# Mask products, two normalisations and a rank rule moved between engines in a two-layer graph kernel

## What is computed

```python
# layer 0, three convolutions, per graph
h = h @ W + b
nh = h / max(norm(h), 1e-12)
ew = adj * (nh @ nh.T)
h = ew @ h                      # relu after the first two

# layer 1 starts with a sequential thinning of the adjacency, row by row
num = sum(row)
sf = (num + 1) // 2 if num > 10 else 1
rank = cumsum(row)
rm = row & (rank % sf == 0)     # only where the node is valid and num > 1
carry[n, :] &= ~rm
carry[:, n] &= ~rm
```

## Time and profile before

| | |
|---|---|
| median of three runs | 2725.25 us (2724.58 to 2729.75) |
| profiled execution, its own time | 2730.12 us |
| its span | 2728.3 us |
| granted TensorE clock, mean | 0.988 |
| busy over the span: PE | 2589.2 us (95%) |
| PE weight loads | 1639.6 us (60%) |
| DVE | 2156.8 us (79%) |
| ACT | 1301.0 us (48%) |
| POOL | 838.1 us (31%) |

### The profile page before, as it was taken

How to read it: one execution, slowest core, us unless ns; L and a number is a source line. 1 busy time by engine, 2 the same in 40 slices (tenths; PEclk the granted TensorE clock), 3 DMA queues, 4 the chain that set the end, 5 groups by cost and what they waited for, 6 DMA issues and landing times. The chain is left out here.

```text
span 2728.3 us, 38640 instructions
## 1 busy us (share of the span) xinstructions
PE 2589.2 (95%) x12390; PEld 1639.6 (60%) x12390; DVE 2156.8 (79%) x5387; ACT 1301.0 (48%) x3804; POOL 838.1 (31%) x449
## 2 busy tenths in 40 slices
PE   7999989999897998989999998999999999999898
PEld 5666656656554665656665554555555555555797
DVE  5889999989889888889989967766666635776676
ACT  3657536555553665455653411322223344444576
POOL 0000050210255003031102120866666613343663
PEclk9999999999998999999999999999999999999999
DMA  7264184363286347056327134355555519997663
GB/s 242 78 182 130 44 196 146 86 183 106 62 208 165 84 124 214 14 156 190 97 86 193 39 72 146 117 198 195 200 200 200 201 62 346 401 401 284 239 233 154
DMA packets 325876, 455.46 MB, mean 167 GB/s; under 512 B 155680, under 2 KB 218528, under 8 KB 325664
## 3 DMA queue, kind: packets, MB, share of 16 engines
q1 hardware_dynamic: 325664, 452.89, 51.9%
HBM read 352.13 MB, written 67.11 MB: 154 GB/s over the span
## 5 line engine op out<-in xcount | busy, mean ns | idle before, releaser
L730 PE MATMUL a_acc<-a_ew,a_Hr 128*128 128x512 f32 x1536 | 752.8, 602 | 0.0
L569 POOL TENSOR_TENSOR a_kp<-a_T,stage 128x512 fp8e4<-128x512 fp8e4 x216 | 275.8, 1288 | 1332.5 <-DMA stage<-a_T 747.1
L900 DVE TENSOR_TENSOR a_ew<-adj,a_cos 128x512 f32<-128x512 f32 x768 | 507.4, 680 | 60.7 <-PE a_cos L723 59.1
L721 PE MATMUL a_cos<-a_nh 128*128 128x512 f32 x768 | 418.5, 545 | 29.4 <-DVE a_ew L900 20.3
L730 PEld LDWEIGHTS a_acc<-a_ew,a_Hr 128*128 128x128 f32 x1536 | 276.7, 191 | 161.1 <-issue 113.4
L835 ACT ACTIVATE a_v<-a_D,a_wb,a_small 128x256 f16<-128x256 f32 x512 | 288.0, 634 | 104.1 <-PE a_D L763 100.6
L825 ACT ACTIVATE a_vr<-a_D,a_small 128x128 f16<-128x128 f32 x560 | 210.5, 458 | 208.1 <-DVE a_small L977 207.6
L723 PE MATMUL a_cos<-a_nh,a_nl 128*128 128x512 f32 x768 | 307.1, 400 | 0.0
L722 PE MATMUL a_cos<-a_nl,a_nh 128*128 128x512 f32 x768 | 304.8, 397 | 0.0
L1385 PE MATMUL b_acc<-adj,b_z 128*128 128x512 f32 x512 | 225.0, 592 | 0.0
L1482 PE MATMUL b_acc<-adj,b_z 128*128 128x512 f32 x512 | 222.5, 592 | 0.0
(11 more groups left out here) (269 smaller groups left out, 4344.5 us busy)
## 6 DMA issues: line engine op xcount, KB each, us to landing
adj<-in_adjT SPq DMA_DIRECT2D x108, 1024.0 KB, 12.7
adj<-in_adjT SPq DMA_DIRECT2D x128, 512.0 KB, 4.0
stage<-in_adj SPq DMA_DIRECT2D x256, 256.0 KB, 3.2
scr_keep<-a_kp SPq DMA_DIRECT2D x256, 64.0 KB, 2.0
scr_z<-b_zT SPq DMA_DIRECT2D x32, 512.0 KB, 3.9
scr_ag<-b_a SPq DMA_DIRECT2D x32, 512.0 KB, 3.2
stage<-scr_keep SPq DMA_DIRECT2D x13, 1024.0 KB, 7.9
b_kp<-scr_keep SPq DMA_DIRECT2D x12, 1024.0 KB, 8.2
```

The lines of the kernel that those rows point to most:

```text
L569: e.tensor_tensor(as_blocks(kp[c % 3][:]), row_half(slot, j, q), turned[:, :, :, :, q % 2], ALU.mult, saturate=False).then_inc(T[done], 1)
L721: e.matmul(cos[j][:], n[:, blk(k)], n[:, half(j)], start=True, stop=False)
L730: e.matmul(acc[j][:], Hr[u % 2][:, k, :], ew[idx % EW][:], start=(k == 0), stop=(k == NK - 1)).then_inc(E["agg"], 1)
L900: e.tensor_tensor(ew[idx % EW][:], adj[g % 2][:, k, half(j)], cos[j][:], ALU.mult).then_inc(E["ew"], 1)
```

## The change

Four things change, all in the first stage:

- All 256 mask products are DVE instructions; POOL has none and runs nothing in the stage. Their planned cost is 620 instead of 700 (DVE) or 1150 (POOL), their rank 3 instead of 1.
- The scaling of `hd` and of `lnb` is eight ACT instructions of 128 x 128 each with the scale (and in `lnb` the bias) as a per-partition operand, planned at 1610. DVE keeps the reciprocals and makes the bias of `lnb` with one more small instruction.
- The rule works on a quarter of the count and needs nine instructions instead of ten. The halving that one of them did is gone; `base` gets one small instruction more.
- `PACE` is 24 instead of 25, so that the dilation's blocks may start somewhat later; planned costs of `rule`, `base` and `wide` are adjusted.

```diff
-PACE = 25
+PACE = 24
...
-def masker(quad, q, j):
-    late = max(q | 1, 4 * j + 3) == NK - 1
-    return "dve" if quad > 1 and late and q % 2 else "pool"
...
-            add("dve", ("lnb", g), 2280, 1, [("act", "lna", g)] + ([("pe", "hf", 0)] if g == 1 else []))
-            add("pe", ("lnc", g), 880, 0, [("dve", "lnb", g)] + bank)
+            add("dve", ("lnb", g), 400, 1, [("act", "lna", g)])
+            add("act", ("lnb", g), 1610, 0, [("dve", "lnb", g)] + ([("pe", "hf", 0)] if g == 1 else []))
+            add("pe", ("lnc", g), 880, 0, [("act", "lnb", g)] + bank)
...
-        add("dve", ("hd", v), 1373, 1, [("act", "hc", v)])
-        add("pe", ("hf", v), 880, 0, [("dve", "hd", v)])
+        add("dve", ("hd", v), 210, 1, [("act", "hc", v)])
+        add("act", ("hd", v), 1610, 0, [("dve", "hd", v)])
+        add("pe", ("hf", v), 880, 0, [("act", "hd", v)])
...
-        add("dve", ("base", n), 190, 2, [("pe", "base", n)], None, None, "D1")
+        add("dve", ("base", n), 320, 2, [("pe", "base", n)], None, None, "D1")
...
-            add("dve", ("rule", n, r), 1290, 3, ...
+            add("dve", ("rule", n, r), 1140, 3, ...
...
-                add("act", ("wide", n, i, j), 900, 1, ...
+                add("act", ("wide", n, i, j), 960, 1, ...
...
-                        add(e, ("mask", quad, i, q, j), 1150 if e == "pool" else 700, 1, ...
+                        add("dve", ("mask", quad, i, q, j), 620, 3, ...
...
+                elif kind == "lnb":                       # ACT
+                    g, = a
+                    x = xt if g in (1, G) else tmp
+                    e.wait_ge(E["lnm"], g + 1)
+                    if g in (1, G):
+                        e.wait_ge(E["tnh"], 3 * g if g == G else 1)
+                    for k in range(NK):
+                        t = e.activation(tmp[:, k, :], x[:, k, :], ACT.Identity, bias=lnnm[:, k:k + 1],
+                                         scale=lnrs[:, k:k + 1])
+                    t.then_inc(E["lnr"], 1)
...
+                elif kind == "hd":                        # ACT
+                    u, = a
+                    e.wait_ge(E["rn"], u + 1)
+                    for k in range(NK):
+                        t = e.activation(tmp[:, k, :], Hr[u % 2][:, k, :], ACT.Identity, scale=rn[:, k:k + 1])
+                    t.then_inc(E["vn"], 1)
...
-                    for k in range(NK):
-                        t = e.tensor_scalar(tmp[:, k, :], x[:, k, :], lnmv[:, k, 0:1], lnrs[:, k:k + 1],
-                                            ALU.subtract, ALU.mult)
-                    t.then_inc(E["lnr"], 1)
+                    e.scalar_tensor_tensor(lnnm[:], lnmv[:, :, 0], -1.0, lnrs[:], ALU.mult, ALU.mult).then_inc(E["lnm"], 1)
...
-                    e.wait_ge(E["rn"], u + 1)
-                    e.tensor_tensor(tmp[:], Hr[u % 2][:], bc(rn[:], 128), ALU.mult).then_inc(E["vn"], 1)
...
+                    e.tensor_scalar(quarter[n // NK % 2][:], ..., 0.5, 0.25, ALU.mult, ALU.add).then_inc(T["b1"], 1)
...
-                    e.scalar_tensor_tensor(c[:], D0[:, :, 127], 0.5, base[p][:, :, 1], ALU.mult, ALU.add)
-                    e.tensor_scalar(m["t"], c[:], 0.5, 0.5, ALU.add, ALU.mult)
-                    e.tensor_scalar(m["sf"], m["t"], MAGIC, MAGIC, ALU.add, ALU.subtract)
+                    e.scalar_tensor_tensor(c[:], D0[:, :, 127], 0.25, quarter[p][:], ALU.mult, ALU.add)
+                    e.tensor_scalar(m["sf"], c[:], MAGIC, MAGIC, ALU.add, ALU.subtract)
...
-        run(nc, pe, act, dve, pool, sp)
+        run(nc, pe, act, dve, None, sp)
```

More of the change, by code:

```diff
@@ L379, in agg @@
         if i == 2 and idx % 16 == 11:
-            read = [("dve", "lnb", G)] if g == G - 1 else []
-            transfer(("xload", g), 1400, read + ([("dma", "postb", UNITS.index((g - 1, 2)))] if g else [("dve", "lnb", 1)]))
+            read = [("act", "lnb", G)] if g == G - 1 else []
+            transfer(("xload", g), 1400, read + ([("dma", "postb", UNITS.index((g - 1, 2)))] if g else [("act", "lnb", 1)]))
     transfer(("xfirst", 1), 1400, (), "sp")
@@ L470, in layer0_plan @@
     quad, i = divmod(ORDER[0], Q)
-    P.transfer(("keep", 0), 2800, [(masker(quad, q, j), "mask", quad, i, q, j) for quad in range(QUADS)
+    P.transfer(("keep", 0), 2800, [("dve", "mask", quad, i, q, j) for quad in range(QUADS)
                                        for i in range(Q) for q in range(NK) for j in range(2)] +
@@ L480, in layer0 @@
         E = P.sems("w xl xld xs tln relu ph hr sq cl nrm rn vn tnh nh nl cos ew agg ev tpost xadd "
-                   "bst bag lnsd lnrs lnr " + " ".join(f"adj{i}{k}" for i in range(2) for k in range(NK)))
-        T = P.sems("at0 at1 fl0 fl1 fl2 fl3 af0 af1 af2 sign low au x bs b0 ct ru vr sd v8 wb wd av rw kpd kpp kps0 kps1 kps2 sum tot flag")
+                   "bst bag lnsd lnrs lnm lnr " + " ".join(f"adj{i}{k}" for i in range(2) for k in range(NK)))
+        T = P.sems("at0 at1 fl0 fl1 fl2 fl3 af0 af1 af2 sign low au x bs b0 b1 ct ru vr sd v8 wb wd av rw kp kps0 kps1 kps2 sum tot flag")
         W, rows = P.sb("W", [128, 3, 128]), P.sb("rows", [128, 3, 128])
@@ L509, in layer0 @@
         base = [P.sb(f"base{p}", [128, Q, 6]) for p in range(2)]
-        cnt = [P.sb(f"cnt{p}", [128, Q]) for p in range(2)]
+        cnt, quarter = ([P.sb(f"{n}{p}", [128, Q]) for p in range(2)] for n in ("cnt", "quarter"))
         wb, own = [P.sb(f"wb{p}", [128, Q, 4]) for p in range(2)], P.sb("own", [128, Q])
@@ L551, in wait_masks @@
         def wait_masks(e, masks):
[L552 to L555, removed]
+            e.wait_ge(T["kp"], max(nth[m] for m in masks))
         def users_of(quad, i, m, j):
[L558 to L570 removed]
+            return [("dve", "mask", quad, i, q, j) for q in (2 * m, 2 * m + 1)]
+        every = [("dve", "mask") + a for a in ring]
         def earlier(engine, kind, upto):
@@ L649, in sp @@
                 e.wait_ge(T[f"kps{c}"], 16 * ((2 * G * NK + 2 - c) // 3))
-        def pool(e):
-            for kind, *a in plan["pool"]:
-                mask(e, *a, "kpp")
         def pe(e):
```

79 lines of the change are left out of this document (38 added, 41 removed).

## The result

Four runs of the changed kernel have a median of 2694.36 us (2690.97 to 2699.59), four of the kernel before on the same chip 2727.5 (2724.58 to 2730.91). The ratio is 0.9879 (95%: 0.9866 to 0.9891): 33 us less. The sign held and the time lies in the forecast range; the gain is half of the 66 us forecast.

The account below looks back on a forecast made before the run. First stage taken as bound by PE and DVE, both near their limit, plus 110 us lost to POOL's stalls. Middle of gains 53 (DVE binds) and 110 (PE binds), 81, less 15 for ACT: 66 us, 2660 us; range 2620 to 2712.

Parts of the forecast that it names:

- 110 us lost where POOL works: First stage: 482 products beside POOL's masks take 1070 us, against 960 us at the pace of stretches nearly without POOL.
- loud stretches: First-stage stretches in which POOL multiplies masks: 2.22 us per product, 2.53 in the worst, against 1.99 elsewhere.
- DVE's added work: First stage, DVE: masks, norms, rule and `base` sum to +51 us, costing 57 us if DVE binds one for one.
- if PE binds, they cost nothing: First stage: with PE as the bound, DVE's 51 us more cost nothing and the gain is 110 us.
- ACT: `hd` and `lnb` sets longer than planned, stopping PE at its transposes: 15 us lost, a quarter of the possible total.
- the 62 us: ACT's total lateness against the plan: 40 us over 48 `hd` sets and 22 us over 17 `lnb` sets.
- Its cover: Stage end: 55 us between the last masks at 1611 us and the last instruction at 1667 make a later block start free.
- Masks' waits in DVE's queue: Rival: masks waiting for transposes or stores hold up DVE's queue, 79 us for 256, slower at 2738 us; chance 0.08.
- PE's pace: Rival: masks fit DVE's gaps and ACT is in time; gain 90 to 115 us, about 2620 us; chance 0.13.
- The stalls are not POOL's: Rival: DVE's stalls have another source, so its work only grows by 25 us, about 2770 us; chance 0.03.
- ACT late: Rival: PE stands at each transpose for 40 to 62 us while DVE binds, 2712 to 2725 us; chance 0.12.
- The dilation ends the stage: Rival: the last mask stays at 1611 us, behind layer 0 at 1600; 45 us won, 2680 us; chance 0.06.

Follow-up runs that it names:

- masks_short: Changed kernel, order kept, all 256 mask products on 16 of every 128 columns (7/8 of the masks left out): 2683.92 us, ratio 0.9839 to the kernel before.
- norms_dve: Changed kernel with the scaling of `hd` and `lnb` back on DVE, masks still on DVE, order planned anew: 2719.06 us, ratio 0.9965 to the kernel before.
- act_short: Changed kernel, order kept, each ACT set of eight scaled copies replaced by one instruction without scaling: 2665.37 us, ratio 0.9779 to the kernel before.
- masks_pool: Changed kernel with masks divided as before (216 on POOL, 40 on DVE), scalings on ACT, order planned anew: 2754.53 us, ratio 1.0090 to the kernel before.
- rule10: Changed kernel with a tenth instruction back in the rule, its planned cost back at 1290, order planned anew: 2703.11 us, ratio 0.9915 to the kernel before.
- pace25: Changed kernel with PACE 25 again, nothing else edited, order planned anew: 2694.73 us, ratio 0.9874 to the kernel before.
- before_pool_short: Kernel before, order kept, only POOL's 216 mask products on 16 of 128 columns, DVE's 40 whole: 2678.66 us, ratio 0.9815 to the kernel before.
- 900: Changed kernel with the planned cost of a mask's store at 900 ns instead of 300, order planned anew: 2674.35 us, ratio 0.9808 to the kernel before.
- 1200: Changed kernel with the planned cost of a mask's store at 1200 ns instead of 300, order planned anew: 2665.52 us, ratio 0.9767 to the kernel before.
- 600: Changed kernel with the planned cost of a mask's store at 600 ns instead of 300, order planned anew: 2696.76 us, ratio 0.9894 to the kernel before.
- both_short: Changed kernel, order kept, ACT sets as one unscaled instruction each and masks on 16 of 128 columns: 2647.71 us, ratio 0.9709 to the kernel before.
- act_cost: Changed kernel with planned costs of ACT's sets at traced lengths (`hd` 2390, `lnb` 2950), order planned anew: 2709.81 us, ratio 0.9939 to the kernel before.

## Why the prediction was right and wrong

**The step that failed** is "110 us lost where POOL works". The mechanism was right and the size was not: in the kernel's own order POOL's masks cost 50 us (56 with DVE's 40 masks cut). The stall itself is nearly the number that I had, 100 us on DVE. I read the difference in pace as its price. That difference held two things: the half of the stall that reached the time, some 50 us, and some 60 us of what makes the loud stretches slow by themselves. Without the stalls the fullest one still takes 2.2 us per product, with PE idle for 10 us and at a clock of 0.97. The other half of the stall cost nothing.

**DVE's added work**, charged at 29 us (half of 57), cost next to nothing. masks_short takes away more than twice as much as it had added up to and wins 10 us. In its place DVE waited longer for PE (115.5 us for 66.0) and for stores, which fits the other end of my step, "if PE binds, they cost nothing". What I missed is the other end of the stage. The dilation's DVE work has a low rank and takes what layer 0 leaves. In norms_dve, with 70 us more of DVE's work by 1600 us, the last `wide` comes 72 us later and masks run behind layer 0. That this is DVE's load and not the order is likely, since PACE and rank did not cure it, but it is not isolated. So the sum over DVE was the wrong account; two ends had to be followed.

**ACT**, 15 us taken between 0 and 62: act_short wins 29 us, and in norms_dve, where ACT has no norms, layer 0 is ready 20 us earlier. masks_pool is 28 us above the kernel before, but it differs in more than its norms. The lengths were nearly right (2.43 and 3.2 us for 2.45 and 2.9); the share of the 62 us that reached the time is up to a half, not a quarter: PE waited at all 48 places and not at 26.

With these the sum is 50 for the stalls less 29 for ACT, 21 of the 33 us. For the rest there are only hints: the shorter rule (9 us by rule10, in an order of its own), DVE's other load (little either way) and the clock, at its lower level for 31 us less. I don't claim that they add up, since each new plan moves both ends by some 10 us.

**Held, and nearly held.** The stalls go. DVE's busy time and the length of the `hd` sets came out as forecast. The pace of 2.15 us in the fullest stretch just misses the "2.1 or less" asked for, and the clock, 1.00 over the stage, is 0.98 in 300 to 600 us and so not 1.00 throughout. PACE was worth nothing (pace25: +0.4 us). Its cover, 55 us before, is 44 us now.

**The rivals.** *Masks' waits in DVE's queue*: real, but 39.2 us / 256 = 0.15 us per mask, where it decides from 0.26 on, so not slower. My argument against it, that DVE's 40 masks had waited 0.31 us each because they shared the ring with POOL's slow ones, does not hold: with POOL's products cut to a quarter those 40 waited 15.8 us in before_pool_short, 0.40 each, and not less than 12.3. They run late in the stage, where masks come close together. Whether the 20 to 29 us won with 900 and 1200 are these waits or a luckier order is not settled: 600 takes 10 us of waits away and wins nothing. *PE's pace* (2620): not reached; both_short, with DVE and ACT both relieved, ends at 2648, so PE and the order have more in them than the 1.94 us per product that I made of the plan's costs. The Trainium skill (Perfetto Trace Analysis, Identifying the Most-Contended Engine) judges TensorE's headroom by the share of weight loads, beside the share of peak FLOPs, which I did not work out. Weight loads are 61% of the stage and DVE is busy for 84%, by which DVE would be the engine to relieve. The runs do not agree: 119 us of DVE's work were worth 10. *The stalls are not POOL's*: ruled out by the lengths above, and by before_pool_short. *ACT late*: right in kind, but at most 29 us and not 40 to 62. *The dilation ends the stage*: not in this kernel, but in six of its neighbours, which makes it the wall next to it.

## What to carry to other kernels

Where two chains share an engine, follow both to where they end: time is the later end, and work taken from the engine is worth something only on the chain that is last. Neither the length of a stall nor the pace of the stretch in which it lies is its price, since other work and other waits lie there too: here half of the stall came back. Under a written-out order the planned costs are a setting of their own: the true lengths of ACT's sets made the kernel 15 us slower, and a store cost that is no truer (1200 ns) was worth nearly as much as the whole change. So an edit that also plans anew should be judged against several orders, or with the order kept. And when a wait names a DMA, look at what the queue that issues it was doing: here it was issuing a transpose.

## What the runs showed of the hardware

A mask product on POOL with an eighth of the columns takes 305 ns for 1163 ns (medians of before_pool_short and masks_pool), on DVE 220 for 685: a quarter and a third, not an eighth. A lone chain of masks goes at two in 2.39 us, though each product is 0.69 us; in that time SP is taken up by issuing one transposing DMA (1.19 us) and two stores (1.05 us together). Eight copies with a scale on ACT take 2.43 us where one DVE product over the same tile took 1.23 (58.8 us for 48, in norms_dve), and one ACT instruction over the same 128x1024 without a scale takes 1.06 us (act_short). The granted clock in 700 to 900 us was 0.94 before, 0.97 with POOL's products cut and 1.00 in the changed kernel, with PE busy for 172, 190 and 187 us; but rule10 and act_cost, with nothing on POOL, have 0.97 there as well. What sets it was not tried.
